# The last half's probabilities turned by TensorE, and the attention bias added by GpSimd in the last head

## The reference

```python
x = x + _layernorm(attn(_layernorm(x)))
x = x + _layernorm(ffn(_layernorm(x)))

# attn: w = codes * repeat(scales, 32, axis=0) for q, k, v, o
q, k, v = y @ wq + bq, y @ wk + bk, y @ wv + bv      # 16 heads of 128
scores = q @ k.T / sqrt(128); attn = softmax(scores)
return (attn @ v) @ wo + bo
# ffn: softmax router over 8 experts, the best 2 kept, silu(x@Wg) * (x@Wu) @ Wd
```

## Time and profile before

| what | value |
|---|---|
| median of 3 runs | 2101.6 us |
| the profiled execution, its own time | 2106.23 us |
| span of its instructions | 2104.5 us |
| granted TensorE clock over the span | 0.986 |
| TensorE busy | 2035.6 us, 97% |
| VectorE busy | 1775.5 us, 84% |
| ScalarE busy | 1404.8 us, 67% |
| GpSimd busy | 1546.5 us, 73% |

### The profile page before, as it was taken

How to read it: one execution, slowest core, us unless ns; L and a number is a source line. 1 busy time by engine, 2 the same in 40 slices (tenths; PEclk the granted TensorE clock), 3 DMA queues, 4 the chain that set the end, 5 groups by cost and what they waited for, 6 DMA issues and landing times.

```text
span 2104.5 us, 32745 instructions
## 1 busy us (share of the span) xinstructions
PE 2035.6 (97%) x11188; PEld 1755.3 (83%) x11188; DVE 1775.5 (84%) x2651; ACT 1404.8 (67%) x2575; POOL 1546.5 (73%) x1329
## 2 busy tenths in 40 slices
PE   7999999999999999999999999999999999849998
PEld 5888888888888888888888888888888888738887
DVE  6889889988989888988999898989898889865553
ACT  5777767776777667776776677776777677624443
POOL 2679778886879777877787787877797678846333
PEclk9999999999999999999999999999999999969999
DMA  4667657766667666765777666766676567730000
GB/s 101 159 154 177 160 141 164 171 164 161 147 155 177 154 146 159 180 159 140 165 169 160 148 160 151 176 154 148 153 181 157 136 151 171 165 112 1 11 11 21
DMA packets 216584, 298.24 MB, mean 142 GB/s; under 512 B 44897, under 2 KB 85345, under 8 KB 216417
## 3 DMA queue, kind: packets, MB, share of 16 engines
q1 hardware_dynamic: 216416, 296.15, 59.9%
HBM read 25.46 MB, written 2.10 MB: 13 GB/s over the span
## 4 chain that ended last, share of the span: by engine, by line
PE 74%; SPq 8%; DVE 7%; POOL 5%; ACT 3%; DMA 2%; issue 1%; POOLq 0%; DVEq 0%; ACTq 0%
PE ps_a L617 16%; PE ps_s L498 13%; PE ps_s L500 13%; PE ps_s L499 13%; PE ps_a L618 8%; SPq L317 7%; POOL pT_both L410 4%; PE ps_a L498 2%; PE ps_a L500 2%; PE ps_a L499 2%; DVE probs L1086 2%; ACT probs L821 2%; DVE part_max L1067 1%; PE ps_a L751 1%; PE ps_a L754 1%
## 5 line engine op out<-in xcount | busy, mean ns | idle before, releaser
L410 POOL TENSOR_TENSOR pT_both<-pT,pT_both 128x512 fp32r<-128x512 f32 x1024 | 1301.1, 1301 | 350.4 <-ACT pT_both L834 348.2
L617 PE MATMUL ps_a<-pT_both,v_hi 128*128 128x512 f32 x2048 | 741.5, 395 | 3.8 <-POOL pT_both L410 3.6
L834 ACT ACTIVATE pT_both<-pT 128x512 fp32r<-128x512 f32 x1024 | 610.7, 630 | 195.5 <-DMA pT<-probs 163.2
L821 ACT ACTIVATE probs<-ps_s,shift 128x1024 f32<-128x1024 f32 x512 | 566.3, 1109 | 259.0 <-DVE shift L1076 258.5
L1086 DVE STREAM_TRANSPOSE probs<-probs 128x1024 f32<-128x1024 f32 x512 | 619.1, 1229 | 55.0 <-ACT probs L821 54.2
L1067 DVE TENSOR_REDUCE part_max<-ps_s 128x1 f32<-128x1024 f32 x512 | 612.4, 1215 | 16.1 <-PE ps_s L500 9.5
L618 PE MATMUL ps_a<-pT_both,v_lo 128*128 128x256 f32 x2048 | 574.5, 281 | 0.0
L617 PEld LDWEIGHTS ps_a<-pT_both,v_hi 128*128 128x128 f32 x2048 | 385.3, 188 | 86.8 <-POOL pT_both L410 3.7
L498 PE MATMUL ps_s<-kT_hi,qT_hi 128*128 128x512 f32 x1024 | 405.0, 396 | 11.6 <-ACT probs L821 8.2
L500 PE MATMUL ps_s<-kT_hi,qT_lo 128*128 128x512 f32 x1024 | 403.6, 394 | 0.0
L499 PE MATMUL ps_s<-kT_lo,qT_hi 128*128 128x512 f32 x1024 | 403.0, 394 | 0.0
(11 more groups left out here) (159 smaller groups left out, 2859.5 us busy)
## 6 DMA issues: line engine op xcount, KB each, us to landing
pT<-probs SPq DMA_DIRECT2D x2048, 128.0 KB, 2.5
pT<-in_L_attn_x SPq DMA_DIRECT2D x4, 512.0 KB, 5.7
codes<-in_L_attn_wk_codes SPq DMA_DIRECT2D x16, 128.0 KB, 2.4
scales<-in_L_attn_wk_scales SPq DMA_DIRECT2D x64, 32.0 KB, 3.0
codes<-in_L_attn_wo_codes SPq DMA_DIRECT2D x16, 128.0 KB, 2.3
scales<-in_L_attn_wo_scales SPq DMA_DIRECT2D x64, 32.0 KB, 1.9
x<-in_L_attn_x SPq DMA_DIRECT2D x4, 512.0 KB, 7.1
layer_out<-x SPq DMA_DIRECT2D x8, 256.0 KB, 2.1
```

Source lines behind the costliest of these rows:

```text
L410: pool.tensor_tensor(pT_lo[:, p, :].rearrange("p (i n) -> p i n", i=Q4), pT[:, s % 2, g, :, t:t + 2, :].rearrange("p i t q -> p i (t q)"), ...
L617: nc.tensor.matmul(out_both, v_hi[:, k, h % 2, :], both[:, :, :, t, :], start=k == 0, stop=False)
L821: nc.scalar.activation(out, src, ACT.Exp, bias=shift[:, s % SLOTS, r:r + 1], scale=SCALE, accum_out=sums[:, s % SLOTS, r, g:g + 1])\
L834: nc.scalar.activation(pT_hi[:, p, :].rearrange("p (i n) -> p i n", i=Q4), pT[:, s % 2, g, :, t:t + 2, :].rearrange("p i t q -> p i (t q)" ...
```

## The change

Four things are altered.

1. **The last half's turn.** For w = 127 `exps` writes the probabilities in their natural order. VectorE's four transposes, the 16 transfers, and GpSimd's `probs_lo` fall away. TensorE transposes 32 tiles of 128 x 128 in four units of eight (`turn_last`), into the ring that held the scores: three units in pass 127 ahead of `out_proj(124)`, the fourth in pass 128 ahead of `weighted_values(126, 7)`. ScalarE's `probs_hi` and VectorE's new `last_rest` read them there.
2. **The bias sum in the last head.** GpSimd adds `vb_sum` to two tiles of `acc` in each of passes 120 to 127, after its eight `probs_lo` (`add_bias(s)`), and VectorE's `add_out` in the last head waits for it. `finish_chunk` keeps only the moments. Chunks 0 and 1 are both finished in pass 127; the moments of the others are spread over passes 129 and 130.
3. **The last head's output weights a head ahead.** They are loaded in pass 114 and decoded in pass 116, the places that a value load would have. `bias_head` says which head's bias goes into which pass: as before for heads 0 to 14, while head 15 has its `bias_out` in pass 119, `bias_hi` and `bias_lo` in pass 118 and the sum in pass 120.
4. **The expert stage's loads** wait for the transfers of halves 0 to 126 and for the last `turn_last`.

```diff
+        LAST = HALVES - 1
+        TU = PAIRS_KT // 2
+        ring += [("t", LAST, u) for u in range(TU)]
+        def bias_head(n):
+            h, s = divmod(n, NH)
+            if s == 5 and 0 <= h < H - 1:
+                return h
+            return H - 1 if n == NH * (H - 2) + 7 else None
...
+                if s == 2 and h == H - 2:
+                    wait(sp, w_ready["o"], h + 1)
+                    load("o", h + 1)
...
+                if n != LAST:
+                    turn_blocks(n)
...
-            sp.wait_ge(pT_loaded[1], LOADS * HALVES // 2)
+            sp.wait_ge(pT_loaded[1], LOADS * (HALVES // 2 - 1))
+            sp.wait_ge(sm["last_turned"], TU)
...
+            def add_bias(s):
+                pool.wait_ge(sm["vb_done"], H)
+                pool.wait_ge(sm["acc_done"], NH * (H - 2) + s + 1)
+                for t in range(RH * s, RH * (s + 1)):
+                    pool.tensor_tensor(acc[:, t, :], acc[:, t, :], vb_sum[:, :], ALU.add).then_inc(sm["vb_added"], 1)
...
+                if s == 4 and h + 2 == H:
+                    weights("o", h + 1)
...
                 for p in range(PAIRS_KT):
                     probs_lo(n - 2, p)
+                    if p == PAIRS_KT - 1 and h == H - 1:
+                        add_bias(s)
...
+            def turn_last(u):
+                ring_free("t", LAST, u)
+                wait(pe, "p_ready", USES * LAST + (3 if u < TU // 2 else 4))
+                for k in range(4 * u, 4 * (u + 1)):
+                    for r in range(RH):
+                        cols = slice((k % GT) * P, (k % GT + 1) * P)
+                        at = (RH * (k % 2) + r) * P
+                        last = nc.tensor.transpose(turned_pair(k // 2)[:, at:at + P],
+                                                   natural(LAST)[:, r, k // GT, cols], ident[:, :])
+                last.then_inc(sm["last_turned"], 1)
...
+                if n == LAST:
+                    for u in range(TU - 1):
+                        turn_last(u)
                 out_proj(n - 3)
...
-                if s == 5 and inner:
-                    bias_out(h)
+                if bias_head(n) is not None:
+                    bias_out(bias_head(n))
...
                 weighted_values(n - 2, 6)
+                if n == LAST + 1:
+                    turn_last(TU - 1)
                 weighted_values(n - 2, 7)
...
+                if w == LAST:
+                    wait(act, "last_turned", p // 2 + 1)
+                    nc.scalar.activation(pT_hi[:, p, :], turned_pair(p), ACT.Copy).then_inc(sm["p_hi_done"], 1)
+                    return
...
-                if s == 4 and inner:
-                    bias_hi(h)
+                if bias_head(n + 1) is not None:
+                    bias_hi(bias_head(n + 1))
...
+            def last_rest(p):
+                wait(dve, "p_hi_done", PAIRS_KT * LAST + p + 1)
+                V.tensor_tensor(pT_lo[:, p, :], turned_pair(p), full(pT_hi[:, p, :]), ALU.subtract)\
+                    .then_inc(sm["last_lo"], 1)
...
+                if w >= NH * (H - 1):
+                    wait(dve, "vb_added", RH * (w % NH + 1))
...
-                dve.wait_ge(sm["vb_done"], H)
                 for t in range(c * TPC, (c + 1) * TPC):
-                    V.tensor_tensor(acc[:, t, :], acc[:, t, :], vb_sum[:, :], ALU.add).then_inc(sm["vb_added"], 1)
-                for t in range(c * TPC, (c + 1) * TPC):
-                    moments(acc, t, "stat1", "aggr1", ("vb_added", t + 1))
+                    moments(acc, t, "stat1", "aggr1")
...
-                if s == 4 and inner:
-                    bias_lo(h)
+                if bias_head(n + 1) is not None:
+                    bias_lo(bias_head(n + 1))
...
+                if n == LAST:
+                    finish_chunk(0)
+                if n == LAST + 2:
+                    dve.wait_ge(sm["acc_done"], HALVES - 2)
+                    for p in range(3, PAIRS_KT - 1):
+                        last_rest(p)
+                        moments(acc, 2 * TPC + p - 3, "stat1", "aggr1")
                 out_lo(n - 3)
+                if n == LAST + 1:
+                    for p in range(2):
+                        last_rest(p)
+                if n == LAST + 2:
+                    last_rest(PAIRS_KT - 1)
...
-                if n >= HALVES - 1:
-                    finish_chunk(n - (HALVES - 1))
+                if n == LAST:
+                    finish_chunk(1)
+                if n == LAST + 1:
+                    last_rest(2)
+                if n >= LAST + 2:
+                    dve.wait_ge(sm["acc_done"], n - 2)
+                    for t in range(RH * (n - 3 - NH * (H - 1)), RH * (n - 2 - NH * (H - 1))):
+                        moments(acc, t, "stat1", "aggr1")
```

More of the change, by code:

```diff
@@ L165, in sandwich_layer @@
             total_done rinv_ready oproj_ready acc_done q_ready q_hi q_lo k_ready k_hi k_lo v_ready v_hi_done v_lo_done
-            vb_hi_done vb_lo_done vb_ready vb_done vb_added
+            vb_hi_done vb_lo_done vb_ready vb_done vb_added last_turned last_lo
             wr_loaded wr_hi_done wr_lo_done before_set pick_set pick_cut pick_hi_done pick_done combT_zero before_done
@@ L329, in _ @@
                     load("o", 0)
[L330 to L334, removed]
+                if s == 1 and h > 0 and more:
+                    wait(sp, w_ready["k"], h + 2)
                     load("o", h)
+                if s == 2 and h == H - 2:
+                    wait(sp, w_ready["o"], h + 1)
+                    load("o", h + 1)
                 if s == 2 and h + 2 < H:
@@ L339, in _ @@
                 if s == 4 and more:
-                    wait(sp, w_ready["o"], h + 1)
+                    wait(sp, w_ready["o"], h + 1 if h + 2 < H else H)
                     if h + 2 < H:
@@ L404, in probs_lo @@
             def probs_lo(w, p):
-                if not live(w):
+                if not live(w) or w == LAST:
                     return
@@ L422, in _ @@
                     weights("k", h + 1)
-                if s == 2 and h < H:
+                if s == 2 and h < H - 1:
                     weights("o", h)
@@ L547, in ring_free @@
                         wait(pe, "v_lo_done", VU * m + part + 1)
+                    if held == "t":
+                        wait(pe, "last_lo", 2 * part + 2)
             def k_proj(h, b):
@@ L614, in weighted_values @@
                 both = pT_both[:, p].rearrange("p b (i t q) -> p b i t q", i=Q4, t=2)
+                if w == LAST:
+                    out, out_both = ps_a[:, s % 2, 0:HQ], ps_a[:, s % 2, :].rearrange("p (b q) -> p b q", b=2)
+                    both = pT_both[:, p].rearrange("p b (t q) -> p b t q", t=2)
                 for t in range(2):
                     k = 2 * p + t
-                    nc.tensor.matmul(out_both, v_hi[:, k, h % 2, :], both[:, :, :, t, :], start=k == 0, stop=False)
-                    last = nc.tensor.matmul(out, v_lo[:, k, h % 2, :], both[:, 0, :, t, :], start=False,
+                    move = both[:, :, t, :] if w == LAST else both[:, :, :, t, :]
+                    nc.tensor.matmul(out_both, v_hi[:, k, h % 2, :], move, start=k == 0, stop=False)
+                    last = nc.tensor.matmul(out, v_lo[:, k, h % 2, :], move[:, 0], start=False,
                                             stop=k == KT - 1)
                 last.then_inc(sm["pv_done"], 1)
+            def turn_last(u):
[8 more added lines that the diff above has]
+                last.then_inc(sm["last_turned"], 1)
             def out_proj(w):
@@ L855, in q_hi @@
                 wait(act, "q_ready", w + 1)
-                if s == 7:
-                    wait(act, "vb_ready", h + 1)
+                if bias_head(w - 2) is not None:
+                    wait(act, "vb_ready", bias_head(w - 2) + 1)
                 nc.scalar.activation(qT_hi[:, s % 2, :], ps_a[:, (s + 1) % 2, 0:HQ], ACT.Identity,
@@ L1093, in out_lo @@
                 wait(dve, "out_hi", w + 1)
+                if w == LAST:
+                    V.tensor_tensor(oT_rest[:, :], ps_a[:, s % 2, 0:HQ], full(oT_hi[:, :]), ALU.subtract)\
+                        .then_inc(sm["out_rest"], 1)
+                    wait(dve, "out_rest", w + 1)
+                    V.tensor_tensor(oT_lo[:, :], ps_a[:, s % 2, HQ:2 * HQ], oT_rest[:, :], ALU.add)\
+                        .then_inc(sm["out_lo"], 1)
+                    return
                 V.tensor_tensor(oT_rest[:, :].rearrange("p (r i q) -> p i r q", r=RH, i=Q4),
@@ L1188, in _ @@
                     q_lo(n + 1)
[L1189 to L1190 removed]
+                if bias_head(n - 1) is not None:
+                    add_bias(bias_head(n - 1))
                 part_of_max(n, 1, 1)
                 row_shift(n, 1)
[L1193 to L1194 removed]
+                if bias_head(n + 1) is not None:
+                    bias_lo(bias_head(n + 1))
                 turn(n, 0, 1)
```

25 lines of the change are left out of this document (17 added, 8 removed).

## The result

The kernel after took 2100.84 us (median of 20 runs, 2098.99 to 2105.84), the kernel before, run 20 times beside it, 2108.77 us (2100.66 to 2114.15). The ratio is 0.9967 with a 95% interval of 0.9958 to 0.9976: about 7 us less, clear of no difference at all, but within the half per cent that was called no change. The profiled execution of after took 2100.96 us. The forecast was 2094.3 us in a range of 2088 to 2102, and a difference of -7.3 us. So the difference came as worked out, the time lies in the range near its upper end, and it is 6.5 us above the forecast, because the median of three runs that the difference was set against lay 7 us under that of twenty.

What follows compares the result with a forecast made beforehand. TensorE's waits bound the steady part; after 1821.3 other engines pace the drain. The drain's -10.6 us and pass 118's +3.3 gave -7.3: 2098.9 us against the profiled 2106.23, 2094.3 against the median 2101.6, range 2088 to 2102.

Steps and rivals of the forecast that it cites:

- rival 1: Drain: transposes slow at 0.28 us each and TensorE's clock low behind them, 2098.2 us, up to 2099; chance 0.15.
- (a): Drain, turn on TensorE: 24 transposes cost 2.8 us, 2.2 of them filling the wait before `out_proj(124)`, 0.5 new but hidden.
- (b): Drain, GpSimd's rests of half 126: from 1825.4 to about 1835.9, next bound once the 16 transfers go; the gain's source.
- (d): Drain's end: split, `out_proj(127)`, `add_out`, moments end at 1848.2 against 1858.83; chunk 2's adds (4.55 us) gone, partly overlapped.
- (c): Drain, last unit and half 127: last unit turned in 0.9 us, then `out_proj(126)` and five pairs, to 1843.2.
- The loads of the expert stage: After the drain: loads start under 2 us earlier, wanted 10.6 us earlier; cost nothing, covered by the drain's remaining 12 us.
- Pass 118, ScalarE: `bias_hi(15)` at the start of pass 118 holds ScalarE 4.2 us and delays `exps`; TensorE loses 2.2 us.
- Rival 2: Pass 118: slack in ScalarE's and VectorE's queues takes up the wait, only the drain counts, 2090 to 2091 us; chance 0.22.
- Pass 118, VectorE: VectorE's chain, late from `exps` and with `bias_lo(15)` added, makes TensorE lose another 1.6 us at `out_proj(115)`.
- its 0.44 us: Pass 124: with `bias_lo` gone from there, the 0.44 us that `out_proj` waited come back.
- GpSimd's adds: Passes 120 to 126: two adds a pass, 1.4 us, fit in some 2.2 us free on GpSimd; cost nothing.
- Rival 3: Last head: GpSimd's adds wait for VectorE and bound it, 1.7 us a pass, 13.6 in all, 2107.9 us; chance 0.05.

Runs made afterwards that it cites:

- run 20: Not a run's label: part of "run 20 times", the kernel before measured 20 times beside the changed kernel, median 2108.77 us.
- the two later sets: Two sets of follow-up experiments, each on one chip with the kernel before beside it, whose median was 2104.97 us in the first and 2105.72 in the second.
- the triple run: Against the changed kernel, each of the last half's 32 transposes done three times into the same place; ratio to the kernel before 0.9996.
- The turn alone: Against the changed kernel, bias adds back on VectorE and head 15's weights and bias product back in place, only TensorE's turn kept; ratio to before 1.0001.
- four adds: Against the changed kernel, each of GpSimd's bias adds made once more into an unread array, four in a pass; ratio to the kernel before 0.9996.
- the changed kernel run again: The changed kernel with nothing altered, measured again beside the experiments and the kernel before; ratio to the kernel before 0.9982.

## Why the prediction was right or wrong

**The step that failed is the last one, the setting of the difference against a base.** The forecast put -7.3 us against a median of three runs, 2101.6 us, though it had noted that the profiled execution, which all its terms come from, took 2106.23. Twenty runs of the kernel before gave 2108.77, and the two later sets 2104.97 and 2105.72. Beside 2108.77 a forecast of 2094.3 claims 14.5 us, and 7.9 came by the medians and 7.0 by the ratio: half. The 7.3 us of the mechanism were right; setting them against 2101.6 was not. Against the profiled time the same -7.3 gives 2098.9, 2.1 us from the 2100.96 us of the profiled execution of after, and those are nearly the 2.25 us by which that execution was late at `out_hi(112)`. Three runs that spread over 10 us don't fix a median to better than several microseconds. That the time lay in the range at all, 1.2 us from its upper end, is owed to the room left there for rival 1, which did not happen.

The steps of the mechanism, in the order of the forecast:

- **(a) The turn.** 24 transposes were to cost 2.8 us at the full clock: they took 2.78, to 2.7 us after the last `exps`, and filled the wait of `out_proj(124)`. This was right, and rival 1 is refuted: 0.115 us apiece and a granted clock of 1.00, in the triple run too. The Trainium skill ("TensorE: Matmul & The Clock Gate", Part 4: PE-mode transpose) gives some 275 ns for one and says that transposes don't count as busy for the clock. In this trace each of the 32 lasts 0.27 us as well, but the next starts 0.11 us after it, so the page's figure isn't the price of one in a row of them; and nothing like its sentence on the clock shows here, where the clock was at its upper level when they began.
- **(b) GpSimd with half 126.** Rests were to start 4.1 us after the end of the last `exps` and end 14.6 after. They started 4.3 and ended 14.3 after (the forecast's 1835.9 should have been 1836.1 by its own terms): the landing was 0.9 us later than assumed, and a rest took 1.26 us instead of 1.34, probably because VectorE doesn't add beside it. The sentence that the gain comes from here is half right: the transfers' going alone is worth 2.1 us, because VectorE's adds are late next. The forecast named them in step (d) as gone too, but as partly hidden; they are worth 4.1 us alone and 8.6 on top of the turn (35.47 to 26.90), the clock's part included.
- **(c), (d) The end.** `out_proj(126)` was to start 17.7 us after the last `exps` and came 17.8 after (1844.24); the drain was to last 26.9 us and lasted 26.90. That exactness is in part luck: `out_proj(127)` was to start 23.1 us after the last `exps` and came 23.7 after, and what was lost was made up because the slow value taken for it, 1.7 us, was not needed, with the clock at 1.00 (1.0 us from 1850.11 to `add_out` at 1851.13).
- **The loads of the expert stage**, costed at nothing: they begin at 1841.52, and the rest of the span is 245.6 us as before. Right.
- **Pass 118, ScalarE.** Forecast 4.2 us of waiting and 2.2 lost by TensorE; measured 4.02 and 2.10, and shown to be the cause by moving the one call. Rival 2 is refuted.
- **Pass 118, VectorE.** This term was over-sized: another 1.6 us at `out_proj(115)` was forecast, and the wait was 0.74. In all TensorE comes to `out_proj(115)` 3.3 us later than in the kernel before, by the distance from the product's last matmul (11.76 us against 8.46), where 3.8 was forecast. Net the middle lost 2.87 us against 3.3 (3.4 by the forecast's own terms). But 0.6 of what came back isn't the change's. From `out_hi(121)` to `out_hi(123)` took 26.13 us before and 25.15 after; the three matmuls of the bias product, now made in pass 119, are 0.36 of the 0.98, and for the rest the forecast had its 0.44 us "with `bias_lo` gone from pass 124". The turn alone keeps `bias_lo` in pass 124, and there it took 0.28 us in place of 1.43, no wait followed, and the same stretch took 25.51 us. VectorE in the kernel before, then with the turn alone:

```profile
1780.89 1.43 DVE L1162 TENSOR_SCALAR vb_lo<-vb_hi,bias_v 128x128 fp32r<-128x128 f32 x1
```

```profile
1784.26 0.28 DVE L1235 TENSOR_SCALAR vb_lo<-vb_hi,bias_v 128x128 fp32r<-128x128 f32 x1
```

Beside the turn alone, pass 118 and what follows cost 3.5 us, and the 2.87 owe 0.6 to a slow instruction in the one profile of before. `bias_lo` in pass 118, 1.3 us of that step's sum, is worth 0.2 to 0.3 us where `exps` is punctual; no run has a late `exps` without it, so how the lateness divides between the two isn't shown.
- **GpSimd's adds**, costed at nothing: 0.74 us each at the median (1.43 for two in a row), in the gap. Right. Rival 3 is refuted in its price and in its form: GpSimd's overrun isn't paid by TensorE in each pass, but once, in the drain, where its lag ends. How far that holds for a longer overrun than that of four adds was not tried.

The difference by stages, -10.63 + 2.87 - 0.09 = -7.85 us, or -7.2 without the slow `bias_lo` of before, stands against the forecast's -7.3. The ratio's -7.0 us (-5.1 to -8.9) agrees; that of the changed kernel run again, -3.8 us (-1.3 to -6.3), is smaller, and why isn't known.

## What to carry to other kernels

Cut two profiles at instructions that both have, and compare the lengths of the stages, before a difference of spans is explained: here the stages told 3 us apart with certainty while whole spans of the same code drifted by more. When a step is moved ahead in a hand-written order, ask how old the product is that its wait names; one that is made in the same moment holds the whole queue, and some places later in the same queue it costs next to nothing (here `bias_hi`, two `exps` later). Two bounds that lie one behind the other in a drain must be priced together, since either alone gives less than half of what both give.

## What the runs showed that I had not expected

**The same instructions take up to 7 us more or less from run to run.** The stretch to `out_hi(112)` lasted 1662.24 us in one profile and 1669.46 in another. One place where this arises is visible. ScalarE, in the same pass of before, of after and of the changed kernel run again, waits for the same transfers (one fence each):

```profile
1324.60 0.63 ACT L834 ACTIVATE pT_both<-pT 128x512 fp32r<-128x512 f32 x1 [5.07 <-DMA pT<-probs]
```

```profile
1326.49 0.63 ACT L897 ACTIVATE pT_both<-pT 128x512 fp32r<-128x512 f32 x1 [5.73 <-DMA pT<-probs]
```

```profile
1322.31 0.63 ACT L897 ACTIVATE pT_both<-pT 128x512 fp32r<-128x512 f32 x1 [3.36 <-DMA pT<-probs]
```

and TensorE's next scores stood 1.50 us in the first, 2.15 in the second and not at all in the third:

```profile
1327.19 0.50 PE L498 MATMUL ps_s<-kT_hi,qT_hi 128*128 128x512 f32 x1 [1.50 <-ACT probs L821]
```

```profile
1329.08 0.50 PE L529 MATMUL ps_s<-kT_hi,qT_hi 128*128 128x512 f32 x1 [2.15 <-ACT probs L880]
```

In these passes ScalarE waits for 16 transfers ahead of which SyncE issued the load of a value weight (its codes at 1307.67 in the kernel before). I set the starts of all `out_hi` of the nine other profiles beside those of before. The distance is up to 1.7 us at the first of them already. From there it changes by more than 0.3 us in one step only at halves 9 and 10, 25 and 26, 40 to 42, 57, 73 and 74, 89 and 90, and 105 and 106, that is once in 16 halves, in passes 3 to 5 of a head with an odd number; the largest step was 3.2 us, at half 105 with the turn alone. All other places together add less than 0.5 us. Behind `out_hi(112)` no such step was seen but those of the edits, and that stretch repeats well. Why the transfers land up to 2 us sooner or later stays open.

**VectorE pays far more for GpSimd's neighbourhood than GpSimd for VectorE's.** An add of 128 x 256 took VectorE 1.24 us beside GpSimd's rests (4.95 us for four) and 0.36 us once GpSimd was done. On GpSimd the same add took 0.74 us with VectorE at work, and its eight rests 10.7 us beside VectorE's adds and 10.1 without them. GpSimd's neighbourhood isn't all that decides: `bias_lo` took 1.43 us in one profile and 0.28 in another, both times while GpSimd made rests, and no run here shows why.
